# Attention inside a fused transformer block: ScalarE writes the rounded halves of projected queries and keys, GpSimd keeps the two subtractions

## The reference

```python
D, H, HD = 256, 16, 64                       # SMAX = sqrt(256)
q = (_ln(x, lnq_s, lnq_b) @ Wq + bq).reshape(Bq, Sq, H, HD).transpose(0, 2, 1, 3)
k = (_ln(x, lnk_s, lnk_b) @ Wk + bk).reshape(Bq, Sq, H, HD).transpose(0, 2, 1, 3)
v = (_ln(x, lnv_s, lnv_b) @ Wv + bv).reshape(Bq, Sq, H, HD).transpose(0, 2, 1, 3)
scores = jnp.einsum('bhqd,bhkd->bhqk', q, k) / SMAX
p = jax.nn.softmax(scores + mask, axis=-1)
att = jnp.einsum('bhqk,bhkd->bhqd', p, v)
```

## Time and profile before

| | before |
|---|---|
| median of 3 runs | 2664.35 us (2663.83 to 2666.37) |
| span of the profiled execution | 2666.0 us |
| attention phase in it, first scores to the last copy of `ov` | 362.6 to 2110.8 us |
| busy over the whole span | PE 93%, DVE 72%, ACT 63%, POOL 56% |

### The profile page before, as it was taken

The page is one execution under the profiler, slowest core; times in us unless marked ns, Lnnn a source line. Parts: engine busy times, 40 slices in busy tenths (PEclk is TensorE's granted clock), DMA queues, the critical chain, the costliest instruction groups (busy, mean ns, idle before and its releaser), DMA issues. The chain is left out here.

```text
span 2666.0 us, 46632 instructions
## 1 busy us (share of the span) xinstructions
PE 2474.6 (93%) x14544; PEld 2106.5 (79%) x14544; DVE 1920.5 (72%) x3637; ACT 1668.4 (63%) x2887; POOL 1501.1 (56%) x1519
## 2 busy tenths in 40 slices
PE   6999879999999999999999999999999689959998
PEld 5888758788887888878888788787888589848887
DVE  5777547877778777787787877878778667545665
ACT  3444447777777777777777777777777534223333
POOL 2333157676776777767777687677776244312221
PEclk9999889999999999999999999999999889969999
DMA  4222332312232121321222222312221253321111
GB/s 156 80 94 87 151 96 70 105 41 80 63 85 89 40 87 58 93 79 56 71 76 74 79 63 63 105 46 79 63 79 56 90 175 120 95 85 32 48 47 40
DMA packets 133706, 212.85 MB, mean 80 GB/s; under 512 B 12564, under 2 KB 95816, under 8 KB 125000
## 3 DMA queue, kind: packets, MB, share of 16 engines
q1 hardware_dynamic: 133576, 211.48, 25.1%
HBM read 112.88 MB, written 48.25 MB: 60 GB/s over the span
## 5 line engine op out<-in xcount | busy, mean ns | idle before, releaser
L1139 DVE TENSOR_REDUCE a_nmax<-a_sc 128x1 f32<-128x1024 f32 x512 | 626.8, 1224 | 301.8 <-PE a_sc L1208 295.7
L1019 ACT ACTIVATE a_pT<-a_tr 128x512 fp32r<-128x512 f32 x1024 | 558.6, 596 | 297.9 <-PE a_tr L1220 296.2
L1085 POOL TENSOR_SCALAR a_pr<-a_pr,a_rden 128x1024 f32<-128x1024 f32 x512 | 575.1, 1129 | 280.8 <-DVE a_rden L1144 244.5
L1150 DVE TENSOR_TENSOR a_pT<-a_tr,a_pT 128x512 fp32r<-128x512 f32 x1024 | 651.2, 678 | 21.9 <-ACT a_pT L1019 20.2
L1241 PE MATMUL a_ov<-a_pT,a_v_s 128*128 128x512 f32 x2048 | 605.4, 417 | 1.4 <-DVE a_half L1130 1.3
L1025 ACT ACTIVATE a_pr<-a_sc,a_nmax 128x1024 f32<-128x1024 f32 x512 | 574.2, 1121 | 11.8 <-DVE a_nmax L1139 7.8
L1208 PE MATMUL a_sc<-a_k_s,a_q_s 128*128 128x512 f32 x2048 | 562.4, 396 | 19.9 <-DMA a_k_s<-a_k_s 18.9
L1220 PEld LDWEIGHTS a_tr<-a_ident,a_pr 128*128 128x128 f32 x4096 | 469.7, 140 | 135.5 <-DVE a_pT L1150 69.3
L1220 PE MATMUL a_tr<-a_ident,a_pr 128*128 128x128 f32 x4096 | 539.8, 274 | 31.4 <-POOL a_pr L1085 28.6
L1208 PEld LDWEIGHTS a_sc<-a_k_s,a_q_s 128*128 128x128 f32 x2048 | 380.7, 189 | 111.7 <-issue 14.8
L1241 PEld LDWEIGHTS a_ov<-a_pT,a_v_s 128*128 128x128 f32 x2048 | 347.4, 189 | 53.9 <-issue 3.4
(11 more groups left out here) (220 smaller groups left out, 3237.5 us busy)
## 6 DMA issues: line engine op xcount, KB each, us to landing
a_z_s<-zT SPq DMA_DIRECT2D x32, 1024.0 KB, 7.0
a_k_s<-a_k_s SPq DMA_DIRECT2D x64, 512.0 KB, 5.5
a_wqk_s<-w_split SPq DMA_DIRECT2D x64, 256.0 KB, 5.2
a_v_s<-a_v_b SPq DMA_DIRECT2D x16, 1024.0 KB, 4.6
att<-a_ao SPq DMA_DIRECT2D x32, 512.0 KB, 2.7
m_att_in<-att SPq DMA_DIRECT2D x16, 1024.0 KB, 5.5
a_wv_s<-w_split SPq DMA_DIRECT2D x17, 512.0 KB, 3.7
zT<-f_zT SPq DMA_DIRECT2D x8, 1024.0 KB, 3.9
```

The lines of the kernel that those rows point to most:

```text
L1019: act.activation(pT[:, (u // 4) % 2, 0, 4 * part:4 * part + 4, (u % 4) * P:(u % 4 + 1) * P], tr[:, part].rearrange("p (t q) -> p t q", t=4 ...
L1085: pool.tensor_scalar(pr[:, k % NP], pr[:, k % NP], rden[:, k % NP:k % NP + 1], 1.0, ALU.mult, ALU.mult).then_inc(s["normed"], 1)
L1139: dve.tensor_reduce(nmax[:, k % NP:k % NP + 1], sc[:, k % 2], AX.X, ALU.max, negate=True).then_inc(s["negmax"], 1)
L1150: dve.tensor_tensor(to[:, 1], tr[:, part].rearrange("p (t q) -> p t q", t=4), to[:, 0].bitcast(F32), ALU.subtract).then_inc(s["tr_lo"], 1)
```

## The change

For a Q or K piece GpSimd used to make both rounded copies (one for each head, 64 rows each, L1059 and L1062) from `staged`, and then both subtractions (L1066, L1068), with a wait for its own result between any two of the four. Now ScalarE writes the two rounded copies from the PSUM bank into `q_s` or `k_s`, ahead of its copy into `staged`; only the last of the three increments `staged`, for which GpSimd waits before its two subtractions. The wait between the subtractions is gone too. In the pieces ahead of the loop VectorE waits for `staged` rather than for GpSimd's copies. V pieces are as they were.

```diff
-            def stage(kind, n, slot, start):
+            def stage(kind, part, n, slot, pair_slot, start):
...
-                    o = act.activation(staged[:, slot], bank_of(n, start)[:], ACT.Identity, bias=bqk_s[:, "QK".index(kind):"QK".index(kind) + 1])
+                    col = "QK".index(kind)
+                    _, hi, _ = parts_of(kind, part, slot, pair_slot)
+                    for head in range(2):
+                        r = rows_of_head(head)
+                        act.activation(hi[head], bank_of(n, start)[r], ACT.Identity, bias=bqk_s[r, col:col + 1])
+                    o = act.activation(staged[:, slot], bank_of(n, start)[:], ACT.Identity, bias=bqk_s[:, col:col + 1])
                 o.then_inc(s["staged"], 1)
...
-            def split_qk(kind, part, n, slot, pair_slot, nqk, hi_only=False):
-
+            def heads_lo(kind, part, n, slot, pair_slot):
...
                 pool.wait_ge(s["staged"], n + 1)
                 stand_alone(pool, turns)
-                pool.tensor_scalar(hi[0], x0, 1.0, 1.0, ALU.mult, ALU.mult).then_inc(s["head0_hi"], 1)
-                pool.wait_ge(s["head0_hi"], nqk + 1)
-                stand_alone(pool, turns)
-                pool.tensor_scalar(hi[1], x1, 1.0, 1.0, ALU.mult, ALU.mult).then_inc(s["head1_hi"], 1)
-                pool.wait_ge(s["head1_hi"], nqk + 1)
-                if hi_only:
-                    return
                 pool.tensor_tensor(lo[0], x0, hi[0].bitcast(F32), ALU.subtract).then_inc(s["head0_lo"], 1)
-                pool.wait_ge(s["head0_lo"], nqk + 1)
                 pool.tensor_tensor(lo[1], x1, hi[1].bitcast(F32), ALU.subtract).then_inc(s["split"], 1)
                 pool.wait_ge(s["split"], n + 1)
...
                     xs, hi, lo = parts_of(kind, part, n % 2, 0)
+                    dve.wait_ge(s["staged"], n + 1)
                     for x in range(2):
-                        dve.wait_ge(s["head%d_hi" % x], n + 1)
```

More of the change, by code:

```diff
@@ L805, in attention_phase @@
             "const first_z z_in wqk_in wv_in v_in k_dup sc masked negmax exp rden normed tr tr_hi tr_lo "
-            "pj staged head0_hi head1_hi head0_lo v_hi first_split split pv half ov_read att att_out").split()}
+            "pj staged head0_lo v_hi first_split split pv half ov_read att att_out").split()}
         PROJ = {2: ("Q", 0), 5: ("Q", 1), 8: ("K", 0), 11: ("K", 1)}
@@ L995, in _ @@
             for n, (kind, part) in enumerate(FIRST):
-                stage(kind, n, n % 2, True)
+                stage(kind, part, n, n % 2, 0, True)
             def body(it, first, last):
@@ L1027, in body @@
                         if piece_at(it, k):
-                            kind, _, n, slot = piece_at(it, k)
-                            stage(kind, n, slot, False)
+                            kind, part, n, slot = piece_at(it, k)
+                            stage(kind, part, n, slot, (k // STEPS + 1) % 2, False)
             over_iterations(act, body)
@@ L1077, in _ @@
                     split_values(part, n, n % 2, n - 4)
-                else:
-                    split_qk(kind, part, n, n % 2, 0, n, hi_only=True)
             def normalise(u, k):
@@ L1106, in body @@
                             pool.wait_ge(s["normed"], it * ITER + k)
-                            split_qk(kind, part, n, slot, (k // STEPS + 1) % 2, it * 8 + 4 + sum(x is False for x in kinds))
+                            heads_lo(kind, part, n, slot, (k // STEPS + 1) % 2)
             over_iterations(pool, body)
```

## The result

The changed kernel is slower: 2709.72 us median (2708.51 to 2714.16, 4 runs) against 2664.13 (4 runs), ratio 1.0165, 95% interval 1.0151 to 1.018. So +45.6 us where I had predicted +25; the time lies above the range. The profiled execution took 2708.51 us and has a span of 2706.2 us. In every run the span is 2 to 3 us less than the time, so the profile of before, with its span of 2666.0, is of an execution of some 2668 us: 2 us above its three runs, and not inside their range, as stated ahead of the prediction. This moves no reading.

The account below looks back on a forecast made before the run. TensorE bounds the attention phase; others matter only where it waits. New waits for ScalarE's `ov` copy (40.8 + 22.2 us) less GpSimd and key waits (24.8 + 8.8 + 4.3) give +25.1: 2689 us, range 2665 to 2701.

Parts of the forecast that it names:

- The copy out of `ov`: TensorE waits for ScalarE's delayed copy: 1.36 us in steps 3 and 19, 0.74 in 7 and 23; +40.8 and +22.2.
- my doubt about step 7: VectorE's half of the `ov` copy might be what TensorE waited for in step 7, making the prediction wrong.
- E: Time the two new ScalarE activations add to each Q or K piece: 1.36 us, bounds 1.18 to 1.42.
- What GpSimd gives back: TensorE's waits for GpSimd shrink: 24.8 us back in steps 5, 21, 8 and 27, 8.8 in step 11.
- The reason given for step 27: Its 0.56 us wait goes whole, behind new waits of steps 19 and 23 and because GpSimd has caught up.
- The reason given for steps 5 and 21: Behind the new waits of steps 3 and 19, their old waits of 0.44 and 0.40 us go whole.
- some 30 waits would stay, at steps 11 and 14: TensorE's waits for GpSimd in the attention phase fall from 73 to some 30, all at these two steps.
- Step 16: TensorE's wait for the doubled keys of step 11's K piece gets 0.27 us shorter, 4.3 us back in all.
- Sum: Total of the losses and gains: 40.8 + 22.2 - 24.8 - 8.8 - 4.3 = +25.1 us.
- Ahead of the loop: VectorE's wait for a GpSimd copy goes, ScalarE's three activations set the pace; nothing counted, within 1 us either way.
- VectorE becomes the late one: Rival, chance 0.13: late `pT` copies delay VectorE; transposes in steps 10, 13, 26, 29 lose 0.25 us each, 2704.

Follow-up runs that it names:

- e9: Changed kernel, ScalarE's loop head at instruction 431, copy out of `ov` put ahead of the piece in steps 2 and 18: 2654.53 us, ratio 0.9955 to the kernel before.
- e6: Kernel before, rounded halves of the keys alone moved to ScalarE, loop head at 431: 2642.3 us, ratio 0.9908.
- e7: Kernel before, rounded halves of the queries alone moved to ScalarE, loop head at 431: 2689.92 us, ratio 1.0085.
- e10: Kernel before, keys and first query half on ScalarE, second on GpSimd, `ov` copy ahead of the piece in steps 2 and 18, head at 431: 2638.24 us, ratio 0.9899.
- e2: Changed kernel with 17 idle semaphore increments ahead of ScalarE's loop, moving its head from 415 to 431: 2682.2 us, ratio 1.0063 to the kernel before.
- e1: Kernel before with 25 idle semaphore increments ahead of ScalarE's loop, moving its head from 391 to 415: 2687.2 us, ratio 1.0076.
- e11: Changed kernel with 9 idle semaphore increments ahead of ScalarE's loop, head at 423: 2683.88 us, ratio 1.0066 to the kernel before.
- e3: Changed kernel with 105 idle semaphore increments ahead of ScalarE's loop, head at 519: 2688.23 us, ratio 1.0082 to the kernel before.
- e5: Kernel before with 41 idle semaphore increments ahead of ScalarE's loop, head at 431: 2662.41 us, ratio 0.998.

## Why the prediction was off

**The copy out of `ov`, steps 3 and 19, 7 and 23: right.** Forecast "some 60" waits, 1.36 us in steps 3 and 19 and 0.74 in 7 and 23; there are 58 waits, and with the head at 431 these steps are 1.38, 1.35, 0.68 and 0.60 longer. e9 shows that the place behind the piece is the cause: with the order turned the loss of 3 and 19 goes. e6 has no such loss, since no copy of `ov` stands right behind a K piece. The 15 waits that the list puts down to GpSimd's L1064 are those of one place, step 7 (1281.08); L1017 ended at 1280.83, and the `split` that step 7's value matmuls ask for is one of the iteration before, given long ago. So the 15 are waits for ScalarE's copy as well. VectorE's half of the copy, my doubt about step 7, ended at 1279.89 + 0.68 = 1280.57 in this iteration, 0.26 ahead of ScalarE's.

**E: right.** 1.40 against 1.36, bounds 1.18 to 1.42. By the overlap of the Trainium skill ("ScalarE: Activation LUTs", section "What ACT_TABLE_LOAD costs") E would have been 1.23; biased activations of 64x512 out of PSUM start 0.70 apart here and show none of it. Lengths agree, 684 ns against its 707. Over the whole span ScalarE is busy for 167.7 us more (forecast some 174) and GpSimd for 159.0 less (some 160).

**What GpSimd gives back, steps 5, 21, 8, 27 and 11: right within 0.15 us.** The reason given for step 27, that GpSimd has caught up, is in part argued: e6 gains 0.60 there without any new wait of TensorE, by the relief in the keys' pieces; e7 gains as much with its own K piece unrelieved, but behind the new waits of steps 19 and 23. The reason given for steps 5 and 21 fits e9 and e10: without the new waits of 3 and 19 they gain 0.24 to 0.29, about the 0.27 that the prediction gives to a place with no such wait, and not the whole 0.44 and 0.40. That some 30 waits would stay, at steps 11 and 14, was wrong: step 11 is 0.64 shorter and shows none.

**Step 16: right in the shifted kernel (-0.24 for -0.27), wrong in the unshifted (+0.10).** There the way from the issue of the doubling DMA (1301.25) to the scores (1308.66) takes 7.41 us, in e2 7.07. So the 0.34 us lie behind the split. The longer way came with code transfers in the changed kernel, but e1 has code transfers too and takes 7.06, so their part in it stays open.

**The step that failed is "Sum": its list of terms.** I went through every instruction that the change adds behind a piece, and priced the 24 that it puts ahead of ScalarE's loop and the 16 inside it only as time on the engine. That they move the loop head in the code had no term. The runs show what that cost: steps 1 and 2 are 1.34 us longer in each iteration, 20 us in all, where the sum had nothing; against the best place of the head, which makes them 0.26 shorter, it is 1.60 us an iteration, 24 us. e1 shows it without the change, e2 and e11 with the change and without the effect: ratios 1.0063 and 1.0066, +17 and +18 us, in the predicted range and some 8 below the forecast; 4 of these 8 are the head at its best place (0.26 x 15), 3 are steps 7 and 23. The profile had the hint: ScalarE idle for 1.41 us at the loop head, where nine in ten of its waits for the transposes are 1.1 us or less, and transfers in the instruction queue all through the loop.

**Ahead of the loop** I counted nothing. The first scores came 4.1 us sooner in the changed kernel, 3.5 in e2, but 1.1 and 1.2 later in e3 and e11, which differ from it by idle instructions only. Among the kernels before it is 362.6, 364.0 (e1) and 364.6 (e5). So these 4 us can't be put down to the change, and my "within 1 us either way" was narrower than the scatter. The end of the program from the last scores on took 570.3 us against 570.6; over all runs it scatters from 565.4 to 571.3.

**The rival "VectorE becomes the late one"** did not come: steps 26 and 29 are unchanged, steps 10 and 13 take 0.09 each in place of 0.25.

## What to carry to other kernels

Ask of an instruction that is added to an in-order engine what stands right behind it in the queue and how much slack that has, not how busy the engine is: the same 1.4 us cost 1.4 behind the first Q piece, 0.6 to 0.7 behind the second and 0.1 behind a K piece, and 0.45 of it was left behind the first Q piece when the urgent copy was put first into idle time. With the head at 431 throughout, moving only the pieces with slack, the keys, makes an iteration 1.24 us shorter than in the kernel before (107.77 against 109.01), and moving all makes it 1.46 longer (110.47); that is some 19 us off and 22 on. And before a difference of a per cent is put down to the edit, shift the loop in the code by some idle instructions and see whether it stays: here a shift alone was worth 27 us (2709.72 against 2682.2, by the ratios too), 24 of them at the loop head.

## What the hardware showed that I had not expected

ScalarE's loop of 259 to 275 instructions ran without any transfer of code, once it had gone round, with its head at 423 or 431, and with five transfers an iteration at 391, 403, 415 and 519. At 415 this costs 1.6 us an iteration over the best place, at 391, 403 and 519 0.2 to 0.3. Why these places differ was not settled. Each transfer is one packet of 8192 bytes (0.76 MB / 93).

The Trainium skill, "Runtime: NRT & Kernel Launch", section "Instruction fetch mechanics", says that a taken branch to code outside the engine's window has to wait for a fetch by DMA. The trace agrees where there are transfers: of the 1.22 us of idle time behind the branch in the changed kernel 0.65 are more than in e2, and 2.18 us come some instructions later. It does not show why a loop of the same length does without at other places. The page has the code come in blocks of 16 KiB; on this queue a packet has half of that, and inside the loop each starts by itself, the next one 0.7 us or more behind it. Here the measurement decides.

The profile did not name the wait for code: it read as a wait for a row maximum that had ended 2.9 us before. The sign of it is that discrepancy of times.
